# Rows of B over the partitions by DMA through a scratch in HBM, in a fused Mamba, feed-forward and minGRU kernel

## What is computed

```
x_dbl = u @ W_x
dt_r, Bm, Cm = x_dbl[..., :8], x_dbl[..., 8:24], x_dbl[..., 24:]
dt = jax.nn.softplus(dt_r @ W_dt + b_dt)
A  = -jnp.exp(A_log)                     # 256 x 16
def step(hstate, inp):
    dA = jnp.exp(dt_s[..., None] * A)
    hstate = dA * hstate + (dt_s * u_s)[..., None] * B_s[:, None, :]
    y = jnp.einsum('bdn,bn->bd', hstate, C_s)
```

## Time and profile before

| | |
|---|---|
| median of 3 runs | 1059.09 us (1058.70 to 1060.96) |
| profiled execution, its own time | 1061.22 us |
| span of its instructions | 1059.4 us, mean granted TensorE clock 0.852 |
| busy share of the span | PE 73%, PE weight loads 59%, DVE 76%, ACT 53%, POOL 49% |
| DMA | 8.39 MB on the queue that SP issues to, 2.9% of the 16 engines' span |

### The profile page before, as it was taken

One profiled execution on the slowest core, in us unless ns is written; L12 is line 12 of the kernel. 1 busy time (PEld: TensorE's weight loads), 2 busy tenths in 40 slices (PEclk: granted clock), 3 DMA queues, 4 the chain that ended last, 5 costly groups with the idle time before them and its releaser, 6 DMA issues. The chain is left out here.

```text
span 1059.4 us, 12336 instructions
## 1 busy us (share of the span) xinstructions
PE 771.0 (73%) x4122; PEld 628.3 (59%) x4122; DVE 801.9 (76%) x1094; ACT 560.8 (53%) x923; POOL 514.6 (49%) x337
## 2 busy tenths in 40 slices
PE   2445557668868698569966897769956997597884
PEld 1234445546766488447855687548845786376673
DVE  3799579868986899868996899779996899324231
ACT  2555465466635764467545764477446754441502
POOL 2287137533751487237742585238733485224321
PEclk9688856878888899689978899789977997899896
DMA  5100000000000000000000000000000000000000
GB/s 131 48 1 0 11 0 1 1 10 1 1 1 1 11 1 11 1 10 0 10 0 10 0 0 10 0 10 0 10 0 0 1 4 9 0 1 11 1 11 10
DMA packets 16901, 8.86 MB, mean 8 GB/s; under 512 B 5328, under 2 KB 15328, under 8 KB 16864
## 3 DMA queue, kind: packets, MB, share of 16 engines
q1 hardware_dynamic: 16864, 8.39, 2.9%
HBM read 6.29 MB, written 2.10 MB: 8 GB/s over the span
## 5 line engine op out<-in xcount | busy, mean ns | idle before, releaser
L832 DVE TENSOR_TENSOR_SCAN state<-dA,inflow 128x1024 f32<-128x1024 f32 x128 | 292.0, 2281 | 31.0 <-ACT dA L569 30.4
L409 POOL TENSOR_TENSOR inflow<-dtu,b_all 128x1024 f32<-128x1024 f32 x112 | 274.5, 2451 | 75.0 <-ACT b_all L559 73.5
L568 ACT ACTIVATE dA<-dt,decay_c 128x512 f32<-128x512 f32 x128 | 88.4, 690 | 214.7 <-DVE state L832 209.4
L838 DVE TENSOR_TENSOR state<-state,c_ps 128x1024 f32<-128x1024 f32 x128 | 153.3, 1198 | 7.2 <-PE c_ps L1111 6.9
L1118 PE MATMUL y_ps<-ident,state 128*128 128x128 f32 x1024 | 158.1, 306 | 0.5 <-DVE state L838 0.5
L1118 PEld LDWEIGHTS y_ps<-ident,state 128*128 128x128 f32 x1024 | 141.8, 160 | 15.5 <-issue 5.8
L1111 PE MATMUL c_ps<-xd,pick 128*128 128x512 f32 x128 | 71.4, 558 | 97.6 <-DVE state L838 93.6
L1026 PE MATMUL work<-in_hi,wzh_hi 128*128 128x512 f32 x256 | 102.3, 399 | 1.7 <-ACT wide L628 1.4
L1111 PEld LDWEIGHTS c_ps<-xd,pick 128*128 128x128 f32 x128 | 27.7, 216 | 126.1 <-DVE state L838 117.6
L1027 PE MATMUL work<-in_hi,wzh_lo 128*128 128x512 f32 x256 | 101.1, 395 | 0.0
L1028 PE MATMUL work<-in_lo,wzh_hi 128*128 128x512 f32 x256 | 100.9, 394 | 0.0
(11 more groups left out here) (169 smaller groups left out, 1702.2 us busy)
## 6 DMA issues: line engine op xcount, KB each, us to landing
x_tok<-in_x SPq DMA_DIRECT2D x8, 256.0 KB, 2.8
out_x<-x_tok SPq DMA_DIRECT2D x8, 256.0 KB, 2.3
wide<-in_Wz SPq DMA_DIRECT2D x1, 1024.0 KB, 11.3
wide<-in_Wh SPq DMA_DIRECT2D x1, 1024.0 KB, 13.4
skip_f<-in_W SPq DMA_DIRECT2D x2, 256.0 KB, 3.8
dtu<-in_W_in SPq DMA_DIRECT2D x1, 256.0 KB
x_tok<-in_w_up SPq DMA_DIRECT2D x1, 256.0 KB, 2.9
x_tok<-in_w_down SPq DMA_DIRECT2D x1, 256.0 KB, 3.1
```

What stands on the lines that cost most here:

```text
L409: pool.tensor_tensor(inflow[:, n % 2, :, :], dtu[:, :, :], b_all[:, n % 2, :].unsqueeze(1).broadcast_to([P, HALVES, SEQ]), ALU.mult).then_ ...
L568: act.activation(dA[:, 0, :], dt[:, 0, :], ACT.Exp, scale=decay_c[:, 0, n:n + 1])
L832: dve.tensor_tensor_scan(flat(state[:, n % 3, :, :]), flat(dA[:, :, :]), flat(inflow[:, n % 2, :, :]), 0.0, ALU.mult, ALU.add).then_inc(s_ ...
L838: dve.tensor_tensor(state[:, n % 3, :, :], state[:, n % 3, :, :], c_ps[:, :].unsqueeze(1).broadcast_to([P, HALVES, SEQ]), ALU.mult).then_i ...
```

## The change

ACT copies the rows 0 to 31 of `b_ps` (B and C, one row per partition) once per sequence into a corner of `b_all`, behind `xd`. SP stores the 16 rows of B to a scratch of 16x512 in HBM, waits until they have landed, and then loads each row back into all 128 partitions (`partition_broadcast`), 256 KB in SBUF per load, 16 loads per sequence. `b_all` gets four buffers (`RING`); load n waits until inflow n-4 has read its buffer. The selector matmuls for B, and the copies of them on DVE and ACT, are gone. To make room in SBUF, `x2b_tok` becomes `x2_tok` itself (the bias is added in place, and waits until `n_tok` of norm 2 has been made), `wdt_f` moves into `dtu`, and the raw ternary weights into `mixed`.

```diff
         dtu = sb("dtu", [P, HALVES, SEQ])
-        b_all = sb("b_all", [P, 2, SEQ])
+        b_all = sb("b_all", [P, RING, SEQ])
+        b_row = b_all[0:2 * STATE, RING - 1, :]
+        b_dram = nc.dram_tensor("b_scratch", [STATE, SEQ], F32).ap()
...
-        x1_tok, x2_tok, x2b_tok = (sb(n, [P, TILES, D]) for n in ("x1_tok", "x2_tok", "x2b_tok"))
+        x1_tok, x2_tok = (sb(n, [P, TILES, D]) for n in ("x1_tok", "x2_tok"))
+        x2b_tok = x2_tok
...
+            def b_store(b):
+                sp.wait_ge(s_brow, b + 1)
+                sp.dma_start(b_dram[:, :], b_all[0:STATE, RING - 1, :]).then_inc(s_bstored, 16)
+                sp.wait_ge(s_bstored, 16 * b + 16)
+
+            def b_load(b, n):
+                if n >= RING:
+                    sp.wait_ge(s_inflow, STATE * b + n - RING + 1)
+                else:
+                    wait(sp, s_inflow, STATE * b)
+                sp.dma_start(b_all[:, n % RING, :], b_dram[n, :].partition_broadcast(P)).then_inc(s_bring[n % RING], 16)
...
-            for i in range(1, FIRST_FULL + 1):
-                load_x(i)
+            def of_round(i, loads, stores):
+                b_store(i)
+                for n in range(RING):
+                    b_load(i, n)
+                if loads:
+                    load_x(i + 1)
+                for n in range(RING, STATE - 1):
+                    b_load(i, n)
+                if stores:
+                    store(i, i - 3)
+                b_load(i, STATE - 1)
...
             def mix_inflow(b, n):
 
-                pool.wait_ge(s_ball, STATE * b + n + 1)
+                pool.wait_ge(s_bring[n % RING], 16 * (STATE // RING * b + n // RING + 1))
                 pool.wait_ge(s_scan, STATE * b + n - 1)
...
+                pool.wait_ge(s_ntok[2], t + 1)
                 pool.tensor_tensor(x2b_tok[:, :, :], x2_tok[:, :, :], bo_tok[:, :, :], ALU.add).then_inc(s_x2b, 1)
...
                 act.activation(xd[:, :], b_ps[:, :], ACT.Copy).then_inc(s_xdhi, 1)
+                wait(act, s_inflow, STATE * b)
+                act.activation(b_row, b_ps[0:2 * STATE, :], ACT.Copy).then_inc(s_brow, 1)
...
-            def mix_b(b, n):
-
-                act.wait_ge(s_bps, STATE * b + n + 1)
-                act.wait_ge(s_inflow, STATE * b + n - 1)
-                act.activation(b_all[:, n % 2, :], b_ps[:, :], ACT.Copy).then_inc(s_ball, 1)
...
-            def mix_b(b, n):
-                dve.wait_ge(s_bps, STATE * b + n + 1)
-                dve.tensor_copy(b_all[:, n, :], b_ps[:, :]).then_inc(s_ball, 1)
...
-            def mix_bn(b, n):
-                if n:
-                    pe.wait_ge(s_ball, STATE * b + n)
-                pe.matmul(b_ps[:, :], pick[:, n:n + 1].broadcast_to([P, P]), xd[:, :], start=True, stop=True).then_inc(s_bps, 1)
```

More of the change, by code:

```diff
@@ L47 @@
 SLOTS = BACK + 4
+RING = 4
 GATE_SLOTS, KEEP_SLOTS, NEW_SLOTS = (4, 5, 7, 9), (4, 6, 8, 10), (5, 6, 8, 11)
@@ L176, in build @@
         win_f = dtu[:, 0, :]
+        wdt_f = dtu[:, 1, 0:INNER]
         w12_f = flat(skip_f[:, 0:2, :])
         wzh_f = flat(wide[:, :, :]).rearrange("p (k n) -> p k n", k=FB)
-        up_raw, up_sign = x2_tok, x2b_tok
-        down_raw, down_sign = flat(x3_tok[:, :, :]), flat(x1_tok[:, :, :])
+        up_raw, up_sign = (mixed[:, k, :].rearrange("p (k d) -> p k d", k=FB) for k in (0, 1))
+        down_raw, down_sign = mixed[:, 2, :], mixed[:, 3, :]
         below = flat(n_tok[:, :, :])
@@ L218, in build @@
         s_dt, s_dtu, s_zero = sem("dt_ready"), sem("dtu_ready"), sem("zero_ready")
-        s_bps, s_cps, s_ball = sem("b_full"), sem("c_full"), sem("b_copied")
+        s_brow, s_bstored, s_cps = sem("b_row_ready"), sem("b_stored"), sem("c_full")
+        s_bring = [sem("b_ring%d" % k) for k in range(RING)]
         s_dA, s_inflow, s_scan, s_read, s_acc = (sem("decay_ready"), sem("inflow_ready"), sem("scan_done"),
@@ L346, in _ @@
             sp.dma_start(wzh_f[:, :, FF:2 * FF], Wh.rearrange("(k p) n -> p k n", p=P)).then_inc(s_w_zh, 16)
-            for i in range(1, FIRST_FULL + 1):
-                load_x(i)
+            def of_round(i, loads, stores):
[9 more added lines that the diff above has]
+                b_load(i, STATE - 1)
+            for i in range(FIRST_FULL):
+                of_round(i, True, False)
             with sp.Fori(FIRST_FULL, ROWS - 1) as i:
-                load_x(i + 1)
-                store(i, i - 3)
-            for i in range(ROWS - 1, ROUNDS):
+                of_round(i, True, True)
+            of_round(ROWS - 1, False, True)
+            for i in range(ROWS, ROUNDS):
                 store(i, i - 3)
@@ L360, in _ @@
             pool.memset(wx_rep[:, :, :], 0.0).then_inc(s_wxz, 1)
-            pool.memset(wdt_f[:, :], 0.0).then_inc(s_wxz, 1)
+            pool.memset(wdt_f, 0.0).then_inc(s_wxz, 1)
             pool.memset(ones[:, :], 1.0).then_inc(s_const, 1)
@@ L405, in mix_inflow @@
             def mix_inflow(b, n):
[L407 removed]
+                pool.wait_ge(s_bring[n % RING], 16 * (STATE // RING * b + n // RING + 1))
                 pool.wait_ge(s_scan, STATE * b + n - 1)
                 pool.tensor_tensor(inflow[:, n % 2, :, :], dtu[:, :, :],
[L410 removed]
+                                   b_all[:, n % RING, :].unsqueeze(1).broadcast_to([P, HALVES, SEQ]), ALU.mult
                                    ).then_inc(s_inflow, 1)
@@ L705, in prepare_mix @@
                 dve.tensor_copy(win_hi[:, :], win_f).then_inc(s_win_hi, 1)
-                dve.tensor_copy(wdt_hi[:, :], wdt_f[:, :]).then_inc(s_wdt_hi, 1)
+                dve.tensor_copy(wdt_hi[:, :], wdt_f).then_inc(s_wdt_hi, 1)
                 dve.wait_ge(s_win_hi, 1)
@@ L709, in prepare_mix @@
                 dve.wait_ge(s_wdt_hi, 1)
-                dve.tensor_tensor(wdt_lo[:, :], wdt_f[:, :], wdt_hi[:, :].bitcast(F32), ALU.subtract
+                dve.tensor_tensor(wdt_lo[:, :], wdt_f, wdt_hi[:, :].bitcast(F32), ALU.subtract
                                   ).then_inc(s_wdt, 1)
@@ L817, in mix_inflow @@
                 dve.wait_ge(s_dtu, b + 1)
-                dve.wait_ge(s_ball, STATE * b + n + 1)
+                dve.wait_ge(s_bring[n], 16 * (STATE // RING * b + 1))
                 if n == 0:
@@ L1051, in mix_ht @@
                 pe.wait_ge(s_htok, b + 1)
-                wait(pe, s_ball, STATE * b)
+                wait(pe, s_xdlo, b)
+                wait(pe, s_brow, b)
                 for j in range(TILES):
@@ L1124, in mix_gt @@
                 if isinstance(b, int) and b == ROWS - 1:
-                    pe.wait_ge(s_ball, STATE * b + STATE)
+                    pe.wait_ge(s_xdlo, ROWS)
+                    pe.wait_ge(s_brow, ROWS)
                 else:
```

13 lines of the change are left out of this document (removed).

## The result

The changed kernel takes 1085.72 us (median of 4 runs, 1083.92 to 1086.08) against 1059.05 for the kernel before: a ratio of 1.0245, with a 95% interval of 1.0227 to 1.0262. The forecast of 1080 us, slower, with a range of 1057 to 1092, holds it; the sum was 5.7 us too small. The profiled execution of the changed kernel took 1083.92 us, with a span of 1082.0. Two labels ahead have to be put right. The round that rows 3 to 7 and the prediction call round 4 is, counted from 0 as the code does, round 5 (its scans begin at 594.33 us). And the 14 us of the earlier trace rows, 636.00 to 650.00, are its slots 13 to 15, not 12 to 14. In the changed kernel its scans begin at 601.58; I stay with this round and call it the same round.

A forecast was written before the change was run, and what follows sets the result against it. DVE was taken as the bound in slots 4 to 19; +3.4 us in each of four loop rounds (+13.6), +5.1, +2.3, -0.65, +1.4 and -1.05 gave +21 on 1059.1: 1080 us, range 1057 to 1092.

The forecast's parts named there:

- DVE bounds slots 4 to 19; PE's and ACT's 130 us are worth nothing: In slots 4 to 19 DVE is the bound; the 67.9 and 64.7 us busy on PE and ACT lie beside its work.
- No change of clock in slots 12 to 14: PE, busy 14.00 of 14.00 us there, keeps clock 1.00 though three or four matmuls of 0.5 us go.
- a clock of 0.50 in slots 5 to 14: PE's clock there in the profile after, named beforehand as one sign that the prediction is wrong.
- DVE and POOL exclude each other, and who asks first holds: SBUF-only DVE instructions and POOL's exclude each other; the second waits for what is left of the first, less 0.15 us.
- The four terms: Per loop round, DVE waits for inflows in slots 7 (least sure), 9, 12, 13: +1.35, 1.0, 0.8, 1.15 us; together +4.3.
- Slot 6, -0.25: DVE's read waits for C behind one selector matmul on PE; its removal saves 0.25 us per round, bounds 0 and 0.53.
- Boundary, -0.65: DVE's second copy in slot 2 goes, shortening the path by 0.65 us per round; store and loads cost nothing.
- Round 7, +5.1: As a loop round, but slot 9 only +0.6 us and slot 16 +2.1, where L916 now meets the inflow.
- Round 0, +1.4: The weights' splitting and ternary work has SBUF-only DVE instructions in two slots: 2 x 1.0 - 0.65 us.
- The tail, -1.05: In round 8 L916 no longer meets POOL's bias addition, which comes later: 1.05 us saved on the path.
- only the gains: Rival: inflows still start more than about 1.2 us after their scan, so no blocks come: 1052 us, chance 0.13.
- PE's clock (1130 us): Rival: with idle time, PE's matmuls in slots 12 to 14 run at 1.2 GHz: +50 us, 1130 us, chance 0.04.

The follow-up runs named there:

- e3: Changed kernel with PE's selector matmuls put back at their old places, read by nobody: 1083.48 us, ratio 1.0227 to the kernel before.
- e1: Changed kernel with POOL's inflow n waiting for the decay n-1 in place of the scan, nothing else moved: 1047.67 us, ratio 0.9882 to the kernel before.
- e2: Kernel before, with ACT's copy of B placed ahead of its decay so the inflow is free early, without DMA: 1106.48 us, ratio 1.0455.
- e5: Changed kernel with POOL's inflow n waiting for the first half of the decay n-1: 1104.0 us, ratio 1.0412 to the kernel before.
- e8: e1 with the store of the 16 rows done 13 times, one after the other, before the loads: 1116.68 us, ratio 1.0521 to the kernel before.
- e4: Kernel before plus the one new wait of POOL's bias addition for n_tok of norm 2: 1059.52 us, ratio 0.9992.

## Why the prediction was right, step by step

- *DVE bounds slots 4 to 19; PE's and ACT's 130 us are worth nothing*: right. In the changed kernel L1104 and L559 are gone, and PE's busy time fell only from 771.0 to 766.8 us, as its other matmuls ran at a lower clock (`y_ps` 325 ns, before 306). I had forecast PE 68 us less busy, and ACT 60, which is 53.5 (560.8 to 507.3); DVE's 20 more are 20.8. The Trainium skill's rule in "TensorE: Matmul & The Clock Gate", Part 1, has the direction right: with less work on PE the mean granted clock went from 0.852 to 0.817. But e3, which restores it, prices it at 2.2 us, not the 50 of that rival.
- *No change of clock in slots 12 to 14, and a clock of 0.50 in slots 5 to 14 as a sign of being wrong*: **the sign came, its price did not**. In slots 13 to 15 of rounds 3 to 6 the changed kernel has a granted clock of 0.89 to 0.90, where the earlier trace rows has 1.00. In slot 13 PE waits for the blocked L980, and from 646.40 to 649.82 the clock is 0.50, 1.2 GHz (PE, then the windows of that stretch and of slots 13 to 15):

```profile
646.13 1.84 PE L1265 MATMUL work<-wo_sb,skip_f 128*128 128x128 f32 x8 [1.11 <-DVE mixed L980]
647.76 1.92 PE L1268 MATMUL work<-wo_sb,mixed 128*128 128x128 f32 x8
...
650.53 1.06 PE L1268 MATMUL work<-wo_sb,mixed 128*128 128x128 f32 x8
```

```profile
646.40:649.82 3.42, 3.42 (x18) 3.42 (x18) 3.42 (x3) 1.30 (x2) 2.22 (x2) 0.50 0.14 50
645.92:661.35 15.43, 15.22 (x119) 15.02 (x120) 14.86 (x26) 3.90 (x6) 6.84 (x4) 0.89 0.20 51
```

  PE's order still fits into DVE's, but only by 0.2 of 15.43 us, and in slot 15 of round 6 it no longer did. e1 (no blocks) and e3 (blocks, and the selector matmuls) both have 1.00 in slots 13 to 15 of the same rounds. So it takes the blocks and the missing matmuls together; the prediction had treated the two apart.
- *DVE and POOL exclude each other, and who asks first holds*: shown by e1, e2 and e5 in both directions. The Trainium skill has this rule in "SBUF — State Buffer", section "Who interferes with whom": the port pair that DVE shares with POOL is an exclusive lock, and a DVE instruction with two SBUF inputs, as L980, contends with a POOL instruction that reads SBUF. The trace agrees, with a wait of what is left of the POOL instruction less 0.15 us (2.41, 2.49 and 2.95 above, where the scan alone takes 1.23).
- *The four terms*: forecast 1.35, 1.0, 0.8 and 1.15 for slots 7, 9, 12 and 13; measured 1.23, 1.01, 0.89 and 1.23. Together 4.36, forecast 4.3. The term I called least sure was off by 0.1.
- *Slot 6, -0.25*: right. The slot itself grew by 0.13, and slot 5 ahead of it shrank by 0.36, as the minGRU's scan there takes 1.54 us instead of 1.90, a term that I did not have. With the selector matmuls kept (e3) the pair takes 10.71 us as before, so slot 6 only waits longer by what slot 5 gains, and the -0.23 of the pair is the selector matmul.
- *Boundary, -0.65*: 43.20 to 42.44, -0.76 in this round, -0.5 to -0.8 ahead of the loop's rounds. The number is near, the reason only in part: in e3, where DVE's copy is gone but the selector matmuls are not, 42.89 us are left, so 0.3 of the 0.76 is what went from DVE and ACT, and the rest comes with PE's matmuls. Store and loads cost nothing there: no wait for them appears, and e8 shows 13 us of slack.
- *Round by round*, in us, from the profiled executions. Slots are 4 to 18, the boundary is the one ahead of the round (ahead of round 0, the time from the start to the first scan):

| round | forecast | slots | boundary | together |
|---|---|---|---|---|
| 0 | +1.4 | +3.6 | -1.2 | +2.4 |
| 1 | -0.65 | -0.1 | -1.1 | -1.1 |
| 2 | +2.3 | +1.95 | -2.1 | -0.1 |
| 3 to 6 | +13.6 | +16.7 | -2.5 | +14.2 |
| 7 | +5.1 | +6.4 | -0.6 | +5.8 |
| tail | -1.05 | | | +1.5 |
| sum | +20.7 | | | +22.6 |

  That the sum comes so near is in part luck: rounds 0, 3 to 7 and the tail are 4.9 us over, rounds 1 and 2 2.9 under. In round 2 the three blocks gave 3.6 us (forecast 3.2), but slots 5 and 14 to 17 gave back 1.7, which I had put at nothing. Of the -2.1 ahead of round 2 some 1.5 is not the change but PE's clock: e5, with the same instructions in this boundary, takes 42.64 us at 0.74, the changed kernel 41.16 at 0.79, and before it was 43.22 at 0.74.
- *The loop round*: forecast 119.5 us, measured 119.36, 119.23, 119.12 and, in the last, 118.79, before 115.97, 116.01, 116.00 and 114.46. The last one grew by 4.3 instead of 3.4; there a read in slot 15 waited 1.0 us for PE.
- *Round 7, +5.1*, or 5.75 without its boundary: slots 4 to 18 grew by 6.4. Slot 16 gave 2.2 (forecast 2.1), slots 7 and 9 1.6 and 0.7 (1.35 and 0.6).
- *Round 0, +1.4*: **mis-sized**. Its slots grew by 3.6, where I priced two at 1.0 each. Slot 9 has 0.7, slot 11 has 3.25 (slot 15 gives 0.4 back). In slot 11 two SBUF-only instructions follow each other, and the second meets not an inflow but POOL's next work, which the earlier inflow has let forward:

```profile
75.67 1.77 DVE L756 TENSOR_SCALAR n_tok<-mixed,thr_neg 128x512 f32<-128x512 f32 x1
77.47 2.72 DVE L758 SCALAR_TENSOR_TENSOR mixed<-mixed,thr,n_tok 128x512 f32<-128x512 f32 x1
```

```profile
74.78 2.37 POOL L438 TENSOR_TENSOR inflow<-dtu,b_all 128x1024 f32<-128x1024 f32 x1 [1.30 <-DVE state L852]
77.11 2.53 POOL L410 TENSOR_TENSOR wzh_lo<-wide,wzh_hi 128x1024 fp32r<-128x1024 f32 x1
```

- *The tail, -1.05*: **wrong** in size and in the sum's sign. e4 does not show it on the path, and from the last scan to the end the changed kernel takes 163.98 us, 1.5 more than before, with the same 630 matmuls in the first 160 us of it. The windows, before, after and in e5, whose program is the same from the last scan on:

```profile
896.97:1056.97 160.00, 118.88 (x630) 96.81 (x628) 49.04 (x115) 55.69 (x95) 46.81 (x38) 0.87 0.01 4
```

```profile
918.06:1078.06 160.00, 122.68 (x630) 99.63 (x628) 48.94 (x111) 55.99 (x95) 45.33 (x38) 0.84 0.01 4
```

```profile
937.77:1097.77 160.00, 119.36 (x630) 97.21 (x628) 47.69 (x115) 55.67 (x95) 47.39 (x38) 0.87 0.01 4
```

PE is 3.8 us longer at it, at 0.84 of the clock instead of 0.87. e5 has 0.87 and takes 161.80 us, 2.2 less than the changed kernel with the same instructions. So the 1.5 us are not work that the change adds: this stretch is longer where PE's clock is lower (161.6 to 164.9 us over all runs here, with PE busy 118.9 to 123.1 of the 160 us). What sets the clock there stays open.
- *The sum*: 21 forecast (20.7 before rounding), 26.7 between the medians, 22.7 between the two profiled executions (1061.22 and 1083.92), which lie 2.2 above and 1.8 below their medians. Where the other runs of the changed kernel spent their 1.5 to 2.2 us more stays open.
- *The rivals*: "only the gains", 1052, did not come by itself, but e1 is what it described: once inflows start more than 1.2 us after the scan, it takes 1047.7. PE's clock (1130 us) fell with e3.
